# Key projection of the second cross-attention moved to the end of the first, earlier and smaller key staging, and eight unused products before each attention

## The reference, cut to what matters

```python
x = x + L0_xattn(layernorm(x), ctx, mask)   # cross0: 1024 queries, 6404 keys, masked
x = x + L0_ffn(layernorm(x))                # self0 (1024 keys), then a mixture of 8 experts
x = x + L1_xattn(layernorm(x), ctx)         # self1 (causal), cross1 (6404 keys), feed-forward
x = x + L1_ffn(layernorm(x))                # a mixture of 8 experts
# each attention:
q, k, v = q_in @ Wq, k_in @ Wk, v_in @ Wv
out = softmax(q @ k.T / sqrt(8)) @ v        # for each of the 16 heads
```

## Time and profile before

| | |
|---|---|
| median of 3 runs | 2662.55 us |
| the profiled execution | 2663.5 us, of which its span is 2661.8 us |
| TensorE, VectorE, ScalarE busy | 89%, 87%, 81% of the span |
| mean granted TensorE clock | 0.951 of full speed |
| cross0: first maxima unit to last | 55.0 to 1040.9 us |
| cross1: first scores | 1563.9 us |

### The profile page before, as it was taken

One profiled execution on the slowest core, in us unless ns is written; L12 is line 12 of the kernel. 1 busy time (PEld: TensorE's weight loads), 2 busy tenths in 40 slices (PEclk: granted clock), 3 DMA queues, 4 the chain that ended last, 5 costly groups with the idle time before them and its releaser, 6 DMA issues.

```text
span 2661.8 us, 59106 instructions
## 1 busy us (share of the span) xinstructions
PE 2357.4 (89%) x23035; PEld 736.7 (28%) x23035; DVE 2327.7 (87%) x2618; ACT 2150.3 (81%) x4104; POOL 296.5 (11%) x849
## 2 busy tenths in 40 slices
PE   5899999999999999489758748999999999999986
PEld 2322222222222222222222222222222222222224
DVE  4999999999999996499747759999999999999935
ACT  3599999999999999479617717999999999999971
POOL 3211111201000000200014300000000100000000
PEclk8899999999999999789879978999999999999998
DMA  6011212111111010111121210111001110011000
GB/s 192 22 50 52 56 45 48 58 41 32 39 34 30 30 30 8 63 44 38 35 83 43 65 60 16 30 38 37 30 30 31 39 34 30 30 32 39 9 3 8
DMA packets 73771, 108.75 MB, mean 41 GB/s; under 512 B 13717, under 2 KB 54402, under 8 KB 73498
## 3 DMA queue, kind: packets, MB, share of 16 engines
q1 hardware_dynamic: 68202, 98.21, 12.0%
q0 software_dynamic: 2032, 3.61, 0.9%
q10 hardware_dynamic: 3264, 3.15, 0.4%
HBM read 72.69 MB, written 23.48 MB: 36 GB/s over the span
## 4 chain that ended last, share of the span: by engine, by line
PE 70%; DVE 16%; ACT 7%; issue 3%; SPq 2%; DMA 2%; POOL 1%; ACTq 0%; DVEq 0%
PE ps L1643 69%; DVE maxima L1388 13%; ACT probs L1185 4%; ACT probs L1142 1%; SPq L617 1%; DVE maxima L1345 1%; DMA q_cross<-probs 1%; SPq L547 0%; DVE stats L1281 0%; DMA q_stages<-q_cross 0%; PE ps L1649 0%; SPq L700 0%; DMA k_self<-probs 0%; POOL probs L887 0%; DVE z L1297 0%
## 5 line engine op out<-in xcount | busy, mean ns | idle before, releaser
L1388 DVE TENSOR_REDUCE maxima<-ps 128x1 f32<-128x920 f32 x1792 | 1894.2, 1110 | 96.1 <-PE ps L1643 92.6
L1185 ACT ACTIVATE probs<-ps 128x512 f32<-128x512 f32 (+1 forms) x3264 | 1762.6, 594 | 131.6 <-PE ps L1643 128.8
L1643 PE MATMUL ps<-probs,v_stage 128*16 128x256 f32 x14208 | 1156.0, 392 | 0.7 <-ACT acc_out L1174 0.4
L1643 PE MATMUL ps<-k_stages,q_stages 64*128 64x460 bf16 (+2 forms) x4032 | 754.1, 372 | 156.8 <-DVE maxima L1388 61.7
L1643 PE MATMUL ps<-q_stages,k_stages 64*128 64x512 bf16 (+1 forms) x3712 | 724.7, 380 | 46.1 <-ACT probs L1142 17.7
L1643 PEld LDWEIGHTS ps<-k_stages,q_stages 64*128 64x128 bf16 x4032 | 193.5, 93 | 1014.8 <-issue 566.5
L1643 PEld LDWEIGHTS ps<-probs,v_stage 128*16 128x16 f32 x14208 | 236.5, 94 | 417.6 <-issue 361.0
L1345 DVE TENSOR_REDUCE maxima<-ps 128x2 f32<-128x1024 f32 (+1 forms) x224 | 239.9, 1106 | 67.5 <-PE ps L1643 64.1
L1142 ACT ACTIVATE probs<-ps 128x512 f32<-128x512 f32 x448 | 224.2, 555 | 50.5 <-PE ps L1643 48.7
L1643 PEld LDWEIGHTS ps<-q_stages,k_stages 64*128 64x128 bf16 x3712 | 187.6, 93 | 277.6 <-ACT probs L1185 79.6
L893 POOL COPY v_stage<-by_key 128x400 f32<-128x400 f32 x64 | 33.0, 516 | 970.7 <-PE ps L1643 874.0
(11 more groups left out here) (236 smaller groups left out, 887.9 us busy)
## 6 DMA issues: line engine op xcount, KB each, us to landing
q_stages<-q_cross SPq DMA_DIRECT2D x256, 48.0 KB
k_stages<-k_cross SPq DMA_DIRECT2D x64, 150.2 KB
k_stages<-k_cross SPq DMA_DIRECT2D x64, 150.0 KB
scratch<-acc_out SPq DMA_DIRECT2D x496, 16.0 KB
k_stages<-k_cross SPq DMA_DIRECT2D x64, 100.1 KB
k_stages<-k_cross SPq DMA_DIRECT2D x64, 100.0 KB
q_stages<-q_self SPq DMA_DIRECT2D x60, 96.0 KB
k_cross<-probs SPq DMA_DIRECT2D x12, 384.0 KB, 3.6
```

Source lines behind the costliest of these rows:

```text
L1185: return nc.scalar.activation(probs[0:m, probs_slot(a, j, i), :], ps[0:m, b_bank(a, use), :], ACT.Exp, scale=float(E) ** -0.5)
L1388: nc.vector.tensor_reduce(maxima[:, at, seg:seg + 1], ps[:, A_BANK + 2 * (g % 2):A_BANK + 2 * (g % 2) + 2, 0:a.segment], AX_XY, ALU.max).t ...
L1643: return nc.tensor.matmul(out_, lhsT, rhs, start=start, stop=stop)
```

## The change

The diff has five parts. (1) The 13 key jobs of cross1 move from passes 1 to 13 to steps 20, 22 and 24 of pass 30 and steps 0, 2, ... 18 of pass 31 of cross0. They write two PSUM banks (2 and 3) that the maxima no longer use then. VectorE takes them out (copy, subtraction, copy) instead of ScalarE; GpSimd does one subtraction instead of two; the parts lie in three buffers in the query staging, and SyncE stores all three parts with one DMA. On VectorE and GpSimd the jobs stand between `finish_first` and `finish_second`, and between `sum_first` and `sum_second`. (2) In cross0, SyncE stages side 0 of the first head's keys after it has stored block 9. (3) After self1, SyncE stages only slot 0 of cross1's keys; the others follow in the loop over the queries' slots, as do those of cross0. (4) `keep_busy`: TensorE makes eight float32 products of 128x512, which nobody reads, between the last `split_rest` and the first scores of each of the four attentions. (5) The waits follow: `clear_queries` waits for the stores, ScalarE no longer waits for the key jobs after cross0, VectorE waits for the last subtraction instead of the last store.

```diff
@@ -172,20 +172,17 @@
     a.half_step = 10
-    a.early_step = 8
-    a.early_tile = a.step_tiles[a.early_step + 1][0]
-    a.early_pass = {1 + e: e for e in range(early_jobs)}
+    late = [(a.n - 2, t) for t in range(20, a.steps, 2)] + [(a.n - 1, t) for t in range(0, a.steps, 2)]
+    a.early_at = {at: e for e, at in enumerate(late[:early_jobs])}
     a.uses = [("turn", 0)]
...
                 a.uses.append(("turn", j + 1))
-            if i == a.early_tile and j in a.early_pass:
-                a.uses.append(("early", a.early_pass[j]))
             a.uses.append(("tile", j, i))
...
     a.before = {kind: list(itertools.accumulate((use[0] == kind for use in a.uses), initial=0))
-                for kind in ("turn", "tile", "early")}
+                for kind in ("turn", "tile")}
     n, banks = len(a.max_units), ceil_div(a.key_tiles, 4)
...
@@ -285,9 +282,12 @@
-        early_whole = xT[:, 0:BANK]
-        early_parts = [xn[:, 4 * b:4 * b + 2, :].rearrange("p t d -> p (t d)").bitcast(BF16) for b in range(2)]
-        early_parts.append(z[:, 0:2, :].rearrange("p t d -> p (t d)").bitcast(BF16))
+        EARLY_RING = 3
+        EARLY_BANK = A_BANK + 2
+        early_parts = [qa_stage.rearrange("p s n -> p (s n)")[:, 3 * BANK * b:3 * BANK * (b + 1)] for b in range(2)]
+        early_parts.append(qb_stage[:, 0:2, :].rearrange("p s n -> p (s n)")[:, 0:3 * BANK])
+        early_parts = [parts.rearrange("p (t n) -> p t n", t=3) for parts in early_parts]
+        early_rests = [z[:, QT:NT, :].rearrange("p t d -> p (t d)"), xT[:, BANK:N]]
         def acc_copy(a, j):
...
@@ -550,6 +546,13 @@
         EARLY = cross1.early_jobs
+        def early_stored(e):
+            return sem(f"early_stored{e % EARLY_RING}")
+        def early_all_stored(engine):
+            for e in range(len(EARLY) - EARLY_RING, len(EARLY)):
+                engine.wait_ge(early_stored(e), (e // EARLY_RING + 1) * DMA)
         def acc_free(j):
...
@@ -607,11 +610,12 @@
                                  ).then_inc(sem("rows_in"), DMA)
-            def stage_keys(a, j):
+            def stage_keys(a, j, *sides):
                 h, _ = a.passes[j]
                 dst, done = k_stage(a, j % a.ring), staged(a, j)
-                for side, (first, count) in enumerate(a.side_keys):
+                for side in sides or range(a.sides):
+                    first, count = a.side_keys[side]
                     row = side * SIDE
...
@@ -622,9 +626,8 @@
                 sp.wait_ge(sem("early_part3"), e + 1)
-                for part in range(3):
-                    sp.dma_start(cross1.k_dram[part, :, c0:c0 + n],
-                                 early_parts[part][:, 0:n]).then_inc(sem("early_stored"), DMA)
+                sp.dma_start(cross1.k_dram[:, :, c0:c0 + n].rearrange("a p c -> p a c"),
+                             early_parts[e % EARLY_RING][:, :, 0:n]).then_inc(early_stored(e), DMA)
             def cross_attention(a):
...
@@ -664,9 +667,12 @@
                 for j in range(a.ring):
-                    if a is cross0:
+                    if j >= 1:
                         stage_keys(a, j)
+                    elif a is cross0:
+                        stage_keys(a, j, 1)
                     stage_queries(j)
...
@@ -677,10 +683,13 @@
                         store_out(j - 1)
-                    if j in a.early_pass:
-                        store_early(a.early_pass[j])
                     if j + 1 < a.n:
                         put_maxima(j + 1)
+                    if j >= a.n - 2:
+                        for e in a.early_at.values():
+                            if (e < 5) == (j == a.n - 2):
+                                store_early(e)
             def short_attention(a):
...
@@ -772,6 +781,10 @@
                             load_mask_row()
+                        if i == 9:
+                            wait_stored(sp, a, 0, 8)
+                            stage_keys(a, 0, 0)
                     wait_stored(sp, a, len(a.jobs) - 1 - a.splits, len(a.jobs) - 1)
...
@@ -787,9 +800,8 @@
                     sp.wait_ge(sem("self1_scores"), 2 * len(self1.all_steps) + self1.n)
-                    sp.wait_ge(sem("early_stored"), len(EARLY) * 3 * DMA)
-                    for j in range(cross1.ring):
-                        stage_keys(cross1, j)
+                    early_all_stored(sp)
+                    stage_keys(cross1, 0)
             result = out.rearrange("a (t p) d -> p (a t) d", p=P)
...
@@ -873,11 +885,9 @@
                 _, _, n = EARLY[e]
-                whole = early_whole[:, 0:n]
-                pool.wait_ge(sem("early_taken"), e + 1)
-                nc.gpsimd.tensor_tensor(whole, whole, early_parts[0][:, 0:n], ALU.subtract).then_inc(sem("early_rest"), 1)
+                parts, rest = early_parts[e % EARLY_RING], early_rests[e % 2]
                 pool.wait_ge(sem("early_part2"), e + 1)
-                nc.gpsimd.tensor_tensor(early_parts[2][:, 0:n], whole, early_parts[1][:, 0:n],
+                nc.gpsimd.tensor_tensor(parts[:, 2, 0:n], rest[:, 0:n], parts[:, 1, 0:n],
                                         ALU.subtract).then_inc(sem("early_part3"), 1)
...
@@ -998,17 +1008,18 @@
                         stage_values(a, a.passes[j + 1][0], (j + 1) % 2)
-                    if j in a.early_pass:
-                        split_early(a.early_pass[j])
                     if j + 1 < a.n:
...
                         sum_first()
+                for e in a.early_at.values():
+                    split_early(e)
                 sum_second()
...
                 pool.wait_ge(sem("cross0_scores"), tile_use(cross0, cross0.n - 1, cross0.key_tiles - 1) + 1)
+                early_all_stored(pool)
                 for q in (qa_stage, qb_stage):
...
@@ -1091,28 +1102,6 @@
                 last.then_inc(sem("values_ready"), 1)
-            def take_early(e):
-                _, _, n = EARLY[e]
-                use = early_use(e)
-                act.wait_ge(sem("cross0_scores"), use + 1)
-                if e == 0:
-                    act.wait_ge(sem("expert_consts"), 1)
-                else:
-                    act.wait_ge(sem("early_part3"), e)
-                    act.wait_ge(sem("early_stored"), e * 3 * DMA)
-                src = ps[:, b_bank(cross0, use), 0:n]
-                nc.scalar.activation(early_whole[:, 0:n], src, ACT.Copy)
-                nc.scalar.activation(early_parts[0][:, 0:n], src, ACT.Copy).then_inc(sem("early_taken"), 1)
-            def early_part2(e):
-                _, _, n = EARLY[e]
-                act.wait_ge(sem("early_rest"), e + 1)
-                nc.scalar.activation(early_parts[1][:, 0:n], early_whole[:, 0:n],
-                                     ACT.Copy).then_inc(sem("early_part2"), 1)
             def short_attention(a):
...
@@ -1225,7 +1209,6 @@
                     layer_norm(0, 1)
-                    act.wait_ge(sem("early_part3"), len(EARLY))
                     turned(0)
...
@@ -1377,6 +1360,23 @@
                         first_attended()
+            def split_early(e):
+                _, _, n = EARLY[e]
+                src, parts, rest = ps[:, EARLY_BANK + e % 2, 0:n], early_parts[e % EARLY_RING], early_rests[e % 2]
+                dve.wait_ge(sem("early_psum"), e + 1)
+                if e == 0:
+                    dve.wait_ge(sem("expert_consts"), 1)
+                if e >= 2:
+                    dve.wait_ge(sem("early_part3"), e - 1)
+                if e >= EARLY_RING:
+                    dve.wait_ge(early_stored(e - EARLY_RING), e // EARLY_RING * DMA)
+                link(nc.vector.tensor_copy(parts[:, 0, 0:n], src))
+                ins = tt(rest[:, 0:n], src, parts[:, 0, 0:n], ALU.subtract)
+                ins.then_inc(sem("early_rest"), 1)
+                dve.wait_ge(sem("early_rest"), e + 1)
+                nc.vector.tensor_copy(parts[:, 1, 0:n], rest[:, 0:n]).then_inc(sem("early_part2"), 1)
             def cross_attention(a):
...
@@ -1526,7 +1528,7 @@
             ln_stats(1, x)
-            dve.wait_ge(sem("early_stored"), len(EARLY) * 3 * DMA)
+            dve.wait_ge(sem("early_part3"), len(EARLY))
             ln_apply(0, z, x)
...
@@ -1818,6 +1820,12 @@
                     at_end(1)
+            def keep_busy(a):
+                pe.wait_ge(sem("split_rest"), a.jobs_before + len(a.jobs))
+                for _ in range(8):
+                    mm(ps[:, A_BANK + 3, :], ident[:], by_key[:, 0:4, :].rearrange("p t d -> p (t d)"))
             def take_late(a, copies, bank):
...
@@ -1870,12 +1877,13 @@
                     _, c0, keys = EARLY[e]
-                    use = early_use(e)
                     if e == 0:
                         pe.wait_ge(sem("early_weight_in"), DMA)
-                    bank_free(use)
-                    mm(ps[:, b_bank(a, use), 0:keys], flat(W["k_cross1"]),
-                       ctxT[:, c0:c0 + keys]).then_inc(sem(a.name + "_scores"), 1)
+                        pe.wait_ge(sem(a.name + "_max_read"), a.n * n)
```

(20 more changed lines are left out.)

## The result

The changed kernel takes 2645.37 us (median of 4 runs, 2644.82 to 2647.06), the kernel before 2664.12 beside it: 18.75 us less. The ratio is 0.9932, with a 95% interval of 0.9915 to 0.9949. The forecast was 2638.0, 24.5 us less, with a range of 2626 to 2652. One caution on the kernel before: of its 22 executions beside the experiments, 20 took 2665.07 to 2668.05 us at a mean granted clock of 0.947 to 0.949, and two took 2662.58 and 2662.29 at 0.951, which is also the clock of the profiled one (2663.5), so that profile is not of its usual execution. Two of the four behind the 2664.12 took 2660.16 and 2662.55; against the 2666.5 beside the first experiments the change would be worth 21 us.

The account below looks back on a forecast made before the run. TensorE was taken to carry 70% of the chain of waits, the three engines handing a tie round inside a pass. Terms -20.8 + 8.6 + 2.5 - 2.5 - 12.3 = -24.5 us gave 2638.0 us, range 2626 to 2652.

Parts of the forecast that it names:

- Passes 1 to 13: cross0's passes that lose the key jobs: each falls from 31.74 to 30.09 us, -20.8 us in all.
- The price of a job: Passes 30 and 31 of cross0: each key job delays the next scores by 0.70 us, +8.6 us in all.
- VectorE and the ring: Passes 30 and 31: VectorE's 1.9 us a job and three staging buffers stay hidden; one 2 us wait misses TensorE.
- `finish_second` late: End of cross0: the last job delays VectorE, TensorE waits 2.3 us before the output product; +2.5 us, 0 to 6.
- Side 0 early: Start of cross0: shorter key staging, less half the possible delay of the stores, gives -2.5 us, 0 to -5.
- Slot 0 only: Start of cross1: queries there at 1547.3 instead of scores at 1563.86, by itself 16.5 us earlier.
- The unused products: They take 9.4 us and release cross1's first scores, leaving -12.3 us with slot 0; 0 in the other attentions.

Follow-up runs that it names:

- The doubled product: The changed kernel with each key job's product made twice on TensorE: 2656.32 us, ratio 0.9960 to the kernel before.
- the jobs from step 16: The changed kernel with its key jobs two pairs of steps earlier, from step 16 of pass 30: 2644.39 us, ratio 0.9909 to the kernel before.
- the last version: The changed kernel without unused products, all of cross0's first-head keys staged after the stores, key jobs from step 16: 2631.91 us, 0.9870 to the kernel before.
- slot 0 alone: The kernel before with one edit, only slot 0 of cross1's keys staged ahead of the queries: 2645.57 us, ratio 0.9920.

## Why the prediction was right, and where it was off

*Passes 1 to 13*: right, -20.1 for -20.8, with 30.13 us a pass.

*The price of a job*: the mechanism was right and a term was mis-sized. I took the next scores to start 0.32 + 0.90 + 0.55 = 1.77 after the last; it was 0.32 + 1.06 + 0.56 = 1.94, so a job costs 0.86 and not 0.70. The 0.90 came from products in a run of four; a product alone among others keeps the engine for 1.06 of its record of 1.13. For 12 jobs the 0.16 more come to 1.9 us, about the 1.75 by which the tail was dearer than forecast. The doubled product shows that nothing of it was hidden.

*VectorE and the ring*: VectorE's copy, subtraction and copy took 0.69, 0.69 and 0.43, within my bounds (1.9 as forecast), and the one wait for the ring 1.66 for 2. TensorE wasn't reached: no idle of it is put down to VectorE ahead of the output product.

*`finish_second` late*: right in place; 2.45 us by the jobs from step 16, +2.5 forecast. It was made up otherwise, though: an idle of 1.46 and not 2.3, and 0.92 because the clock fell in it and the product took 2.08 in place of 1.16. In the kernel without products, whose tail of cross0 is the same, VectorE didn't wait for that product at all and the tail took 54.42, so this 0.9 comes and goes, and what the earlier jobs give without it is 1.5 to 1.6 (2.45 - 0.92, and 54.42 - 52.80 in the last version).

*Side 0 early, -2.5*: this step failed; the first scores came 0.9 later. I had halved a delay of the stores between 0 and 4.9 us; it was 5.25 (10.24 for 4.99), more than the upper end, and ate all of the gain. The wait for blocks 0 to 7, which the edit puts ahead of the key copies and so ahead of the next stores too, I had not counted. In the second half of the last store's 10.24 us, the DMA engines are busy a fifth of the time:
```profile
43.00:48.00 5.00, 0.46 (x2) 0.00 (x0) 0.00 (x0) 0.00 (x0) 0.00 (x0) 0.93 0.20 63
```
The Trainium skill, "DMA: Bandwidth & Descriptors", section "Why a DMA increments its semaphore by 16 and not by 1", says that a copy runs only on as many engines, up to 16, as divide its outermost dimension on both sides, and on the lowest-numbered ones. By that rule the three key copies (24, 16 and 8 rows, from 3, 2 and 8) would use 3, 2 and 8 engines, by my estimate, and the stores, which use those too, would wait on them; the trace agrees with it: 0.20 of 16 is about 3 engines busy while a store is held up, and there is no gain in all. No run here shows which engines they were. I had cited the rule and weighed it too lightly.

*Slot 0 only*: better than forecast. The queries are there a us behind VectorE's last subtraction, not at 1547.3. By itself the edit moves the first scores by 17.7 us behind those of self1, with the slower clock of self1's last pass in it, and gives 18.0 in the span and 20.9 in the median, where the forecast's step had 16.5.

*The unused products*: right in what they do. In cross0, self0 and self1 they changed nothing; in cross1 they took 8.79 us for 9.4, part slow and part fast, released the first scores and left the clock up. Their price against none was forecast as 16.5 - 12.3 = 4.2; it is 8.55 - 1.9 = 6.7, since the queries no longer hold the scores. The median without products, 2638.77, is 6.6 lower.

*What no step had*: +2.5 us in self1 from a clock that fell. The kernel with slot 0 alone shows the same fall ahead of its only edit, so it isn't an effect of the change. It is more likely one of the profile of the kernel before, the only one besides the last version in which the clock stayed up there: most executions of that kernel took 3 to 4 us longer than the profiled one, at a mean clock of 0.947 to 0.949 for 0.951. They have no trace, so that they had this fall too is not shown.

The sum, then: -24.5 forecast; side 0 gave 3.4 less, the jobs cost 1.8 more, the passes gave 0.7 less, the clock in self1 took 2.5, and cross1 gave 1.6 more (-13.9 for -12.3): -17.7, and with the 0.3 ahead of self0 the -18.1 of the spans, within rounding.

## What to carry to other kernels

Before a head start is queued ahead of other transfers, ask which transfers share its DMA engines: here it delayed by 5.25 us exactly the last store that its consumer also waited for. Unused work to keep a clock up is worth at most the slow stretch that it removes (1.9 us here) and costs what it delays (8.55); where it closed a gap and delayed nothing, in self0, it gained nothing either. Work put into a stage in which one engine releases the next in turn cost its full time on the path here, however idle the engine looks; price it by the distance to the next start (1.06) and not by its share in a run (0.90). Before a stretch is called lost, compare the profiled execution's time and clock with those of the other executions: here the profile of the kernel before was not of a usual one.

## What the runs showed that was not expected

The clock fell while TensorE was working, not only while it stood still. In eight of the ten profiles it dropped to 1.2 GHz in self1's last pass; in six of these it stayed there for 12 to 14 us (in the other two for 3 and 7), with TensorE busy 12.32 of 13 us in the changed kernel and 10.78 of 12 in the one with slot 0 alone. In the 5 us ahead of 1500 in the changed kernel it had been busy for 3.83; in the same part of the kernel before for 3.91, without a fall. And after an idle it fell late: in self1 of the changed kernel the clock stayed at 1.00 through the 5.18 us without work and dropped when the first scores had begun.
```profile
1370.00:1371.00 1.00, 0.00 (x0) 0.00 (x0) 0.00 (x0) 0.00 (x0) 0.00 (x0) 1.00 0.34 127
1371.00:1372.00 1.00, 0.38 (x5) 0.30 (x5) 0.00 (x0) 0.00 (x0) 0.00 (x0) 0.85 0.23 65
1372.00:1373.00 1.00, 1.00 (x7) 1.00 (x6) 0.42 (x1) 0.00 (x0) 0.00 (x0) 0.50 0.34 125
```
What decides when it falls stays open; no run here tells it.
